# Vision tower kernel: the gate's exponentials on ScalarE and a new order of gated turn, routed products and transform

## What is computed

```python
h = patches(x) @ tok_W                                    # 256 channels
# mixer, on layernorm(h)
x_proj = n @ in_w + in_b
mod = gelu(n @ mod_w1 + mod_b1) @ mod_w2 + mod_b2         # 256 -> 1024 -> 256
y = irfft(rfft(x_proj * mod) * rfft(kernel))              # along the 196 tokens
h = h + y @ out_w + out_b
# low-rank experts, on layernorm(h)
logits = n @ router_W.T + router_b                        # 6 experts
gate = softmax(logits); keep the largest 2
w = gate * kept; w = w / (sum(w) + 1e-6)
h = h + n @ base_W.T + base_b + shared(n) + sum_e w[e] * B[e] (A[e] n)   # rank 16
```

## Time and profile before

| what | value |
|---|---|
| time, median of 3 runs | 1248.16 us (1247.44 to 1250.17) |
| profiled execution | 1247.64 us, of which the span shown is 1245.8 us |
| TensorE busy | 1223.9 us (98%), granted clock 0.999 |
| weight loads busy | 1175.7 us (94%) |
| VectorE busy | 888.8 us (71%) |
| ScalarE busy | 643.2 us (52%) |
| GpSimd busy | 406.9 us (33%) |
| DMA | 72.97 MB, mean 59 GB/s |

### The profile page before, as it was taken

One profiled execution on the slowest core, in us unless ns is written; L12 is line 12 of the kernel. 1 busy time (PEld: TensorE's weight loads), 2 busy tenths in 40 slices (PEclk: granted clock), 3 DMA queues, 4 the chain that ended last, 5 costly groups with the idle time before them and its releaser, 6 DMA issues.

```text
span 1245.8 us, 20849 instructions
## 1 busy us (share of the span) xinstructions
PE 1223.9 (98%) x7914; PEld 1175.7 (94%) x7914; DVE 888.8 (71%) x2591; ACT 643.2 (52%) x1197; POOL 406.9 (33%) x459
## 2 busy tenths in 40 slices
PE   9999999999999999999999999999999999999998
PEld 8899999999999999999999999999999999999996
DVE  6477766677766777766777666777667777667777
ACT  6645555545555445555455555455554445454432
POOL 3523244332244232343232443323442323433220
PEclk9999999999999999999999999999999999999999
DMA  7310222221322111222202222212221112211001
GB/s 244 94 49 20 68 69 68 56 34 47 69 69 68 56 28 55 69 68 56 59 23 68 69 68 56 33 49 68 68 69 55 26 57 68 68 56 33 14 13 34
DMA packets 85089, 72.97 MB, mean 59 GB/s; under 512 B 64775, under 2 KB 78958, under 8 KB 81150
## 3 DMA queue, kind: packets, MB, share of 16 engines
q1 hardware_dynamic: 84990, 71.66, 20.4%
HBM read 43.07 MB, written 12.85 MB: 45 GB/s over the span
## 4 chain that ended last, share of the span: by engine, by line
PE 80%; DVE 9%; ACT 7%; issue 2%; DMA 1%; SPq 1%; POOL 0%; ACTq 0%; DVEq 0%
PE rotating L1457 16%; PE rotating L1458 15%; PE rotating L1459 15%; PE rows_ps L1457 8%; PE rows_ps L1458 6%; PE rows_ps L1459 6%; PE turn L1744 5%; PE turn L1507 2%; PE rows_ps L1517 2%; ACT gelu_h L661 2%; DVE y_l L1161 1%; ACT y_h L698 1%; ACT gelu L656 1%; DVE gelu_l L1106 1%; DVE gated_l L1186 1%
## 5 line engine op out<-in xcount | busy, mean ns | idle before, releaser
L529 POOL TENSOR_TENSOR folded<-modulated 128x196 f32<-128x196 f32 x63 | 38.1, 605 | 565.0 <-DVE modulated L1118 565.0
L656 ACT ACTIVATE gelu<-rotating,consts 128x392 f32<-128x392 f32 x256 | 145.4, 582 | 109.2 <-PE rotating L1459 108.9
L514 POOL TENSOR_TENSOR gelu_l<-gelu,gelu_h 128x784 fp32r<-128x784 f32 x62 | 128.7, 2075 | 213.1 <-DVE norm L1101 172.0
L509 POOL TENSOR_TENSOR patches_l<-patches,patches_h 128x384 fp32r<-128x384 f32 (+1 forms) x186 | 182.1, 1008 | 2.8 <-ACT patches_h L608 2.8
L1457 PE MATMUL rotating<-x_h,w_h 128*128 128x392 f32 x512 | 177.2, 346 | 1.6 <-ACT gelu L656 1.6
L1457 PE MATMUL rotating<-gelu_h,w_h 128*128 128x392 f32 x512 | 177.4, 346 | 0.0
L1458 PE MATMUL rotating<-x_l,w_h 128*128 128x392 f32 x512 | 174.6, 341 | 0.0
L1459 PE MATMUL rotating<-x_h,w_l 128*128 128x392 f32 x512 | 174.6, 341 | 0.0
L1458 PE MATMUL rotating<-gelu_l,w_h 128*128 128x392 f32 x512 | 174.2, 340 | 0.0
L1459 PE MATMUL rotating<-gelu_h,w_l 128*128 128x392 f32 x512 | 174.0, 340 | 0.0
L1457 PE MATMUL rows_ps<-tokw_h,patches_h 128*128 128x256 f32 x570 | 162.9, 286 | 1.5 <-DVE patches_l L871 1.5
(11 more groups left out here) (300 smaller groups left out, 2997.7 us busy)
## 6 DMA issues: line engine op xcount, KB each, us to landing
patches<-dram_x_rest SPq DMA_DIRECT2D x30, 1152.0 KB, 5.2
out<-h_sb SPq DMA_DIRECT2D x30, 384.0 KB, 2.5
prod<-spec_y SPq DMA_TRANSPOSE x60, 3.2
patches<-dram_x_first SPq DMA_DIRECT2D x2, 384.0 KB, 5.7
h_sb<-dram_x_second SPq DMA_DIRECT2D x1, 768.0 KB, 7.6
patches<-dram_x_fourth SPq DMA_DIRECT2D x1, 768.0 KB, 9.6
h_sb<-dram_first SPq DMA_DIRECT2D x2, 320.0 KB, 3.5
gelu<-dram_w SPq DMA_DIRECT2D x1, 512.0 KB, 8.1
```

What stands on the lines that cost most here:

```text
L509: pool.tensor_tensor(patches_l[:, k, 0:n], patches[:, k, 0:n], patches_h[:, k, 0:n].bitcast(F32), ALU.subtract).then_inc(pool_patches_lo, 1)
L514: pool.tensor_tensor(gelu_l[:, 2 * j:2 * j + 2, :], gelu[:, 2 * j:2 * j + 2, :], gelu_h[:, 2 * j:2 * j + 2, :].bitcast(F32), ALU.subtract)\
L529: pool.tensor_tensor(folded[:, m, 0, :, 1:NF], fwd, back, ALU.add)
L656: act.activation(gelu[:, k, :], bank(g + 1, UP[k])[:, 0:GT], ACT.Gelu, bias=b1_bias[:, k:k + 1]).then_inc(act_gelu, 1)
```

## The change

The polynomial is gone. ScalarE runs `ACT.Exp` on the shifted logits in every step; a dummy exponential on three numbers (`gate_table`) stands ahead of it, and the first GELU stands behind it. The ranks compare the shifted logits and not the normalised gates, and the sum over all six only scales the epsilon, so normalising is gone too. VectorE puts both parts of the fold together. On TensorE the gated turn stands behind up block 3 (before: 5), `routed` and `dft` behind up block 5 (before: 6 and 7), `inverse_dft` behind embedding tile 0 (before: 1). ScalarE writes the gated and the fold's high halves ahead of GELU's first high half, and VectorE's low half 2 of GELU stands behind the spectrum's products. The program's end is ordered alike. The diff's core:

```diff
-IN, UP, TURN_GATED, OUT, DOWN = (0, 1), (2, 3, 4, 5, 6, 7, 9, 10), 8, 11, (12, 13)
+IN, UP, TURN_GATED, OUT, DOWN = (0, 1), (2, 3, 4, 5, 7, 8, 9, 10), 6, 11, (12, 13)
# ScalarE
-            def sine_whole(g): ...
+            def gate_table():
+                act.activation(gate_small[:, 7, :], gate_small[:, 1, :], ACT.Exp)
+            def gate_exp(e):
+                act.wait_ge(dve_gate, GATE_STEPS * e + 3)
+                act.activation(gate_wide[:, 1].rearrange("p t e -> p (t e)"),
+                               gate_wide[:, 0].rearrange("p t e -> p (t e)"), ACT.Exp).then_inc(act_gate_exp, 1)
@@ loop, ScalarE
+                if in_range(tail):
+                    gate_table()
+                    gate_exp(tail)
                 gelu_tile(mid, 0)
-                if in_range(back):
-                    sine_whole(back)
                 gelu_tile(mid, 1)
                 gelu_tile(mid, 2)
-                gelu_hi(mid, 0)
                 gelu_tile(mid, 3)
-                gelu_tile(mid, 4)
                 if in_range(tail):
                     gated_hi(tail, bank(i, TURN_GATED))
                 if in_range(back):
                     fold_hi(back)
+                gelu_hi(mid, 0)
+                gelu_tile(mid, 4)
                 gelu_tile(mid, 5)
@@ end of the program, ScalarE
             project(last, range(DH))
+            gate_table()
             fold_hi(last - 1)
+            gate_exp(last - 2)
             gelu_tile(last, 0)
...
@@ VectorE: gate_range, gate_exp and gate are replaced by gate_logits (bias, maximum,
@@ subtraction), gate_ranks (L1086 to L1089 on the shifted logits) and gate_rows
+                dve.wait_ge(act_gate_exp, e + 1)
+                dve.wait_ge(dve_gate, before + 6)
+                dve.scalar_tensor_tensor(out=wide(4), in0=wide(3), scalar=1.5, in1=wide(1), op0=ALU.is_lt,
+                                         op1=ALU.mult).then_inc(dve_gate, 1)
+                dve.tensor_reduce(small(2), gate_wide[:, 1], AX_X, ALU.add).then_inc(dve_gate, 1)
+                dve.wait_ge(dve_gate, before + 7)
+                dve.tensor_reduce(small(3), gate_wide[:, 4], AX_X, ALU.add).then_inc(dve_gate, 1)
+                dve.wait_ge(dve_gate, before + 9)
+                dve.scalar_tensor_tensor(out=small(4), in0=small(2), scalar=GATE_EPS, in1=small(3), op0=ALU.mult,
+                                         op1=ALU.add).then_inc(dve_gate, 1)
...
-            def cosine_whole(g):
+            def join_fold(g):
                 dve.wait_ge(fold_turned, 32 * (g + 1))
-                dve.tensor_copy(whole_halves[0:NF, 0], turned_halves[0:NF, :, 0, :]).then_inc(dve_whole, 1)
+                for x in range(2):
+                    dve.tensor_copy(whole_halves[0:NF, x], turned_halves[0:NF, :, x, :]).then_inc(dve_whole, 1)
@@ loop, VectorE
-                for j in range(0 if i == 1 else 2, 3):
-                    gelu_lo(mid, j)
                 if in_range(back):
                     real_products(back)
                     imaginary_products(back)
                     spectrum_of_y(back)
-                gelu_lo(mid, 3)
+                for j in range(0 if i == 1 else 2, 4):
+                    gelu_lo(mid, j)
@@ loop, TensorE
                 pe.wait_ge(act_gelu, HC * mid + 2)
+                if in_range(tail):
+                    turn_gated(tail, bank(i, TURN_GATED))
+                pe.wait_ge(act_gelu, HC * mid + 3)
                 mlp_up(mid, 4)
-                pe.wait_ge(act_gelu, HC * mid + 3)
+                pe.wait_ge(act_gelu, HC * mid + 4)
                 mlp_up(mid, 5)
-                pe.wait_ge(act_gelu, HC * mid + 4)
-                if in_range(tail):
-                    turn_gated(tail, bank(i, TURN_GATED))
-                pe.wait_ge(act_gelu, HC * mid + 5)
-                mlp_up(mid, 6)
                 if in_range(tail):
                     routed(tail, rows_ps)
-                pe.wait_ge(act_gelu, HC * mid + 6)
-                mlp_up(mid, 7)
                 if in_range(back):
                     dft(back)
+                mlp_up(mid, 6)
+                pe.wait_ge(act_gelu, HC * mid + 5)
+                mlp_up(mid, 7)
...
                 embed(i + 1, 0)
-                embed(i + 1, 1)
                 if in_range(back):
                     inverse_dft(back)
+                embed(i + 1, 1)
```

More of the change, by code:

```diff
@@ L836, in _ @@
             gelu_tile(last, 3)
+            gated_hi(last - 2, bank(GROUPS, TURN_GATED))
             gelu_tile(last, 4)
@@ L839, in _ @@
             gelu_tile(last, 5)
-            gated_hi(last - 2, bank(GROUPS, TURN_GATED))
             gelu_hi(last, 2)
@@ L1015, in over_experts @@
                 return a.rearrange("p (t a) -> p t a", a=1).broadcast_to([P, n, EXPERTS])
[L1017 to L1031, removed]
-                dve.wait_ge(pe_route, e + 1)
[L1033 to L1087, removed]
-                link(dve.tensor_tensor(flat(1), flat(0), room.thr, ALU.is_gt))
-                link(dve.tensor_reduce(room.wide[:, 3], room.cmp[:, 1], AX_X, ALU.add))
-                link(dve.scalar_tensor_tensor(out=wide(4), in0=wide(3), scalar=1.5, in1=wide(2), op0=ALU.is_lt,
-                                              op1=ALU.mult))
-                link(dve.tensor_reduce(small(3), room.wide[:, 4], AX_X, ALU.add))
-                link(dve.tensor_scalar(small(4), small(3), GATE_EPS, None, ALU.add))
-                link(dve.reciprocal(small(5), small(4)))
-                link(dve.tensor_tensor(room.wide[:, 5], room.wide[:, 4], over_experts(small(5), n),
-                                       ALU.mult))
-                assert done[0] == GATE_STEPS - EXP_STEPS
-                hidden = routes[:, 0:n, 0:ROUTED].rearrange("p t (e r) -> p t e r", r=RANK)
-                weight = room.wide[:, 5].rearrange("p t (e a) -> p t e a", a=1)\
-                    .broadcast_to([P, n, EXPERTS, RANK])
-                dve.tensor_tensor(room.gated.rearrange("p t (e r) -> p t e r", r=RANK), hidden, weight,
@@ new lines, in gate_ranks @@
+            def gate_ranks(e):
+                before = GATE_STEPS * e
+                e4 = [P, TILES, EXPERTS, EXPERTS]
+                logits = gate_wide[:, 0]
+                other = logits.rearrange("p t (a e) -> p t a e", a=1).broadcast_to(e4)
+                own = logits.rearrange("p t (e a) -> p t e a", a=1).broadcast_to(e4)
+                flat = lambda c: gate_cmp[:, c].rearrange("p t e f -> p (t e f)")
+                dve.wait_ge(dve_gate, before + 3)
+                dve.tensor_tensor(gate_cmp[:, 0], other, own, ALU.subtract).then_inc(dve_gate, 1)
+                dve.wait_ge(dve_gate, before + 4)
+                dve.tensor_tensor(flat(1), flat(0), rank_thr, ALU.is_gt).then_inc(dve_gate, 1)
+                dve.wait_ge(dve_gate, before + 5)
+                dve.tensor_reduce(gate_wide[:, 3], gate_cmp[:, 1], AX_X, ALU.add).then_inc(dve_gate, 1)
@@ new lines, in gate_rows @@
+            def gate_rows(e):
+                before = GATE_STEPS * e
+                small = lambda c: gate_small[:, c]
+                wide = lambda c: gate_wide[:, c].rearrange("p t e -> p (t e)")
+                dve.wait_ge(act_gate_exp, e + 1)
[8 more added lines that the diff above has]
+                                         op1=ALU.add).then_inc(dve_gate, 1)
+                dve.wait_ge(dve_gate, before + 10)
+                dve.reciprocal(small(5), small(4)).then_inc(dve_gate, 1)
+                dve.wait_ge(dve_gate, before + 11)
+                dve.tensor_tensor(gate_wide[:, 5], gate_wide[:, 4], over_experts(small(5), TILES), ALU.mult)\
+                    .then_inc(dve_gate, 1)
+                dve.wait_ge(dve_gate, before + GATE_STEPS)
+                hidden = round_routes[:, 0:TILES, 0:ROUTED].rearrange("p t (e r) -> p t e r", r=RANK)
+                weight = gate_wide[:, 5].rearrange("p t (e a) -> p t e a", a=1)\
+                    .broadcast_to([P, TILES, EXPERTS, RANK])
+                dve.tensor_tensor(gated.rearrange("p t (e r) -> p t e r", r=RANK), hidden, weight,
@@ L1403, in _ @@
             fold_lo(last - 1)
-            gate_range(last - 2, round_routes, round_room)
-            gate_exp(last - 2, round_room)
-            gate(GATE_STEPS * (last - 2) + EXP_STEPS, round_routes, round_room)
+            gate_logits(last - 2)
+            gate_ranks(last - 2)
+            gate_rows(last - 2)
             real_products(last - 1)
```

47 lines of the change are left out of this document (23 added, 24 removed).

## The result

| | before | after |
|---|---|---|
| time, median of 4 runs | 1248.21 us (1247.44 to 1250.17) | 1212.97 us (1212.12 to 1214.33) |
| profiled execution | 1247.64 us | 1212.12 us |
| one step, mean of 28 | 37.84 us | 36.69 us |

The ratio is 0.9716 (95% interval 0.9700 to 0.9733): the change takes 35.2 us off, where 26 were forecast. The sign and the mechanism were right, the size was not: 1212.97 lies under the range's lower end of 1218. In the session of the last two experiments one of nine executions of the kernel before took 6462 us; it is left out of their comparison.

A forecast was written before the change was run, and what follows sets the result against it. TensorE was taken to bound the kernel, only its queue's stalls being winnable: 27.2 + 0.5 - 1.5 = 26.2 us off the profiled 1247.64, giving 1221.4, as a median 1222 us; range 1218 to 1236.

The forecast's parts named there:

- The three waits: TensorE's weight loads for gated rows' low half, y's low half and spectrum: gone or under 2 us each.
- The gate's chain: Gate on VectorE: links from scaling to normalising leave the chain ahead of the gated rows, 2.84 us shorter.
- The margin at up block 3: TensorE's weight load there, after ScalarE's second table load and first GELU: 0.05 us to spare, zero cost taken.
- Rival A: Exponentials to up block 3: a table switch costs more than its row, 1257 us (1260 by skill page); chance 0.07.
- B: Up block 3, transform, inverse: new chains each miss by a little, 1226 to 1236 us; chance 0.17.
- C: Other waits show up behind the three that leave, most gain lost, 1237 to 1250 us; chance 0.06.
- the bound put on the sum: Sum of the weight loads' own waits on TensorE, 31.9 us, taken as upper bound where 27.2 was kept.
- the inverse: TensorE's stall for the spectrum before the inverse transform goes: 0.18 us a step, 5.4 us in 30.
- the mixer: TensorE's stall for y's low half before the mixer's output products goes: 0.38 us a step, 11.4 us in 30.
- routed products: TensorE's stall for the gated rows' low half before them goes: 0.36 us a step, 10.4 us in 29.
- transform: Its weights on TensorE come late after the fold's low half: 0.05 us a step charged, 1.5 us; bounds 0 and 0.3.
- The second step: GELU wait of 1.45 us goes, transform waits for the same late DMA: even, 1 us either way.

The follow-up runs named there:

- the last two experiments: e9 and e10; the kernel before took 1247.2 to 1249.9 us beside them.
- e6: Kernel after plus a short GELU and a short exponential between the gate's exponentials and first GELU (two more table switches a step): 1337.33 us.
- e7: Kernel after without the dummy exponential (`gate_table`): 1212.61 us, 36.69 us a step.
- e9: Kernel after plus one short ScalarE copy between the gate's exponentials and Gelu's load: 1214.39 us, 36.68 us a step.
- e2: Kernel after with VectorE's order, the inverse's place, routed products and transform (behind blocks 6 and 7) as before; gated turn early: 1240.30 us.
- e3: As e2, but VectorE's spectrum products ahead of its low half 2 of GELU: 1227.36 us, 37.23 us a step.
- e10: Kernel after without the dummy exponential and, in the second step alone, the transform behind up block 7: 1215.84 us, ratio 0.9738.
- e5: Kernel after with its whole order, but the polynomial gate of before on VectorE and no exponentials on ScalarE: 1271.86 us.
- e1: Kernel after with every order of the step put back as before; only the short gate and VectorE's joined fold remain: 1247.53 us.
- e8: As e1, without the wait for ScalarE's sixth GELU right ahead of the mixer's wait: 1245.93 us, 37.83 us a step.

## Why the prediction was right or wrong

**Right.** The three waits are gone, and nothing came in their place. The gate's chain is 2.78 us shorter, where 2.84 was forecast: gated rows ended 624.89 - 619.00 = 5.89 after the gate's start, and end 603.79 + 0.46 - 601.14 = 3.11 after it now. The first GELU ends 1.9 us after the exponentials' end, as forecast; the table load costs its 1.28 and is the only cost of the switch (e6), it stands ahead of the wait (e7). The margin at up block 3, forecast at 0.05, was as narrow as that (e9). The drain that the Trainium skill ("ScalarE: Activation LUTs", section "What ACT_TABLE_LOAD costs") adds to a load shows in no run here, not even where three switches follow each other. Rival A is out. Rivals B and C did not happen either: the range left room above the forecast, and the miss was below.

**Wrong: the size of the terms.** The steps that failed are the prices of two stalls and the bound put on the sum: the inverse was priced at 0.18 us a step and gave 0.30, the mixer at 0.38 and gave 0.46, and the 31.9 us taken as the most that could be won was passed by the loop alone with 33.4. Against the profiled execution the forecast was 1221.4 us, and 1212.1 came. The terms, a step, each as the difference of the mean stretches of TensorE's timeline over 28 steps:

| term | forecast | measured | by 29 steps |
|---|---|---|---|
| routed products | 0.36 | 0.36 | 0.0 |
| inverse | 0.18 | 0.30 | +3.5 |
| mixer | 0.38 | 0.46 | +2.4 |
| transform | -0.05 | 0.02 | +1.9 |
| all else | 0 | 0.01 | +0.3 |
| sum | 0.87 | 1.15 | +8.1 |

The rest of the 9.3 us is the second step (0.5 forecast, 1.5 came), the start (0.2) and the end (0.4 for 0.5).

*The mixer* was read off one step, and that step was a cheap one. In the next step of the kernel before the pause was larger, and over 28 steps it was 0.27 us in eleven and about 0.42 in seventeen:

```profile
676.67 0.28 PE L1459 MATMUL rows_ps<-tokw_h,patches_l 128*128 128x256 f32 x1
677.21 0.39 PE L1457 MATMUL rows_ps<-outw_h,y_h 128*128 128x256 f32 x1 [0.26 <-DVE y_l L1161]
```

0.54 - 0.12 = 0.42 us where the earlier trace rows gave 0.27; the mean over 28 steps is 0.37, and the first product behind it adds about 0.10. The row that groups them was at hand: the weight loads waited 12.2/30 = 0.41 us on the average, and 0.31 in the step that I took. I had used it only as an upper bound.

*The inverse* lost the 0.18 that I counted (0.20 in the mean), and 0.10 more that I did not. Its 16 products stand in one merged row, so the longer first product can't be seen in it; but the distance from the row's start to the next row's can: 1.81 us before, 1.70 after (614.46 to 616.16). I had added such a share to the other two waits and left it out at the third. e2 to e3 gives 0.32 for all of it, since in e2 the pause had grown by 0.03.

*The transform* was charged 0.05 a step, since its weight load would be that late. It was not late. The chain was placed rightly: its low half ended at 607.40 + 1.23 = 608.63, 4.45 us after up block 3's start at 604.18, where 4.47 was forecast. But I had let the weight load stand 0.16 ahead of its product, and it stands 0.11 ahead, 0.12 behind the load before it, as in any other place of this stretch:

```profile
608.70 0.16 PEld L1424 LDWEIGHTS turn<-fold_h,dft_h 99*99 99x99 f32 x1
```

```profile
608.81 0.40 PE L1424 MATMUL turn<-fold_h,dft_h 99*99 99x512 f32 x1
```

The low half ended only 0.07 us before that load. The rows of the kernel before could not tell that so narrow a margin would hold in every step; that it did is in part luck.

*The bound.* I took 31.9 us, the sum of the weight loads' waits, as the most that could be won, and built the lower end of the range on it. It is no bound: part of each wait is slack (0.42 us of wait stood for 0.25 of pause at the routed products), but the product behind each wait also takes about 0.1 us more, which adds some 9 us for 89 waits and stands in no wait. There was a check that I left out: without the three pauses and the longer products behind them the mean step of the kernel before is about 36.7 us, and the step took 37.84. That gives 1.1 us a step.

*The second step* I had put at even. A wait of 1.45 us for a GELU went and one of 1.27 for the fold came, as foreseen, but inverse and mixer there gained about 0.9 and not 0.56.

*Two readings* in the prediction were off without an effect on the time. The links between 619.63 and 622.47 are fourteen, not eleven: the eleven of the polynomial and three for sum, reciprocal and normalising; the 2.84 us are right. And a GELU of 0.59 us does not take less than half of a block's 1.08; only the distance between two that follow each other at once, 0.47 us, does. The GELUs caught up even so.

## What to carry to other kernels

Where one engine's queue bounds a loop, a shorter chain on another engine is worth nothing until the consumer is moved up in the queue, and moving it without the shorter chain can cost more than it wins. Here the gate alone left the mean step where it was, the order alone made the program 24 us slower, and both made it 35 us faster: price the two together. Price a removed wait by the loop's mean, not by one step, and count what stands behind the wait too, the first product whose weight load lies open. Subtracting the step without its waits from the mean step checks the sum. Before an operation is moved away from one partner, look at the distance to its other one (e10).

## What the runs showed of the hardware

- A ScalarE table switch cost 1.28 us and 0.01 to 0.02 of handover wherever it stood, also three in a row (e6), and the load ran ahead of the wait of its activation (e7).
- A weight load 0.04 us late did not move its product (e9); the product behind one that waited visibly took about 0.1 us more (0.39 for 0.28 us), on top of the pause.
- After a stop of 2.8 us in each step TensorE was granted half its clock for 2.3 us or more, which cost 1.5 us a step (e6); stops of 1.9 us in each step left it at 1.00 (e5), one of 1.9 us in the second step was followed by a mean of 0.60 over 4.1 us (e10). What makes the difference is open.
- A second wait instruction right ahead of a late wait made a handover 0.06 us longer (e1 against e8).
